# Attention 3: VectorE adds exponentials of two heads, TensorE sums three blocks of denominators per quad in place of six

## The reference

```python
h = jnp.concatenate([x, latents], axis=1)                 # 1601 + 512 = 2113 keys
q = (latents @ q_w + q_b).reshape(b, k_len, NH, DH)       # 512 queries, 16 heads of 32
kv = (h @ kv_w + kv_b).reshape(b, p + k_len, NH, DH, 2)
attn = jnp.einsum('bkhd,bnhd->bhkn', q, kmat) / DH
attn = jnp.where(full_mask[:, None, None, :], attn, -jnp.inf)
attn = jax.nn.softmax(attn.astype(jnp.float32), axis=-1)
attn_out = jnp.einsum('bkhn,bnhd->bkhd', attn, v)
```

## Time and profile before

| | us |
|---|---|
| median of 3 runs | 5292.15 (5284.46 to 5299.27) |
| profiled execution | 5292.46 |
| its span, first to last instruction | 5290.7 |
| PE busy in the span | 4730.2 (89%) |
| DVE busy | 3685.4 (70%) |
| ACT busy | 2956.0 (56%) |
| POOL busy | 2035.2 (38%) |

### The profile page before, as it was taken

The page is one execution under the profiler, slowest core; times in us unless marked ns, Lnnn a source line. Parts: engine busy times, 40 slices in busy tenths (PEclk is TensorE's granted clock), DMA queues, the critical chain, the costliest instruction groups (busy, mean ns, idle before and its releaser), DMA issues. The chain is left out here.

```text
span 5290.7 us, 75559 instructions
## 1 busy us (share of the span) xinstructions
PE 4730.2 (89%) x28874; PEld 1700.7 (32%) x28874; DVE 3685.4 (70%) x4647; ACT 2956.0 (56%) x5454; POOL 2035.2 (38%) x916
## 2 busy tenths in 40 slices
PE   7978898997797999997899999997789999996899
PEld 2423444443333233332322222222333333331344
DVE  6749999997453877771599999994567777771421
ACT  5644444443221466664388888886336666664432
POOL 1226667664000477884000000000008888885000
PEclk9989999998898799998999999998889999998999
DMA  3343434334011333313111111112424232312100
GB/s 129 131 164 105 108 105 125 113 93 152 24 64 43 73 75 74 78 47 109 66 31 32 33 33 34 34 30 71 118 80 99 59 82 58 69 40 77 64 25 16
DMA packets 474866, 391.91 MB, mean 74 GB/s; under 512 B 175151, under 2 KB 372628, under 8 KB 474472
## 3 DMA queue, kind: packets, MB, share of 16 engines
q1 hardware_dynamic: 474496, 387.00, 27.2%
HBM read 246.50 MB, written 139.34 MB: 73 GB/s over the span
## 5 line engine op out<-in xcount | busy, mean ns | idle before, releaser
L2871 DVE TENSOR_REDUCE att_part<-att_scores 128x2 f32<-128x802 f32 x1024 | 953.7, 987 | 110.0 <-PE att_scores L2710 98.1
L2844 ACT ACTIVATE att_prob<-att_lower 128x512 f32<-128x512 f32 (+1 forms) x1664 | 883.2, 596 | 129.6 <-PE att_lower L2724 108.6
L3678 DVE TENSOR_REDUCE att_part<-att_scores 128x1 f32<-128x423 f32 x1280 | 675.8, 590 | 219.5 <-PE att_scores L3381 219.5
L3622 ACT ACTIVATE att_prob<-att_lower 128x512 f32<-128x512 f32 (+1 forms) x1088 | 563.3, 602 | 243.5 <-PE att_lower L3393 241.6
L3662 POOL TENSOR_TENSOR att_acc<-att_acc,att_prob 128x1024 f32<-128x1024 f32 (+2 forms) x240 | 671.4, 2798 | 51.5 <-ACT att_prob L3622 22.4
L2447 DVE TENSOR_REDUCE att_part<-att_scores 128x1 f32<-128x401 f32 x1024 | 515.5, 567 | 162.0 <-PE att_scores L2261 161.9
L1441 POOL TENSOR_TENSOR scan_z<-scan_r,scan_states 128x512 f32<-128x512 f32 x256 | 469.0, 1836 | 337.2 <-DVE scan_states L1518 324.1
L2739 PE MATMUL att_lower<-att_prob,att_v 128*32 128x256 f32 (+1 forms) x6144 | 523.5, 413 | 19.7 <-issue 19.7
L2386 ACT ACTIVATE att_prob<-att_scores 128x512 f32<-128x512 f32 (+1 forms) x832 | 430.9, 601 | 195.6 <-PE att_scores L2273 195.6
L2858 POOL TENSOR_TENSOR att_out<-att_sums_sb,att_spread 128x512 f32<-128x512 f32 x32 | 40.7, 1273 | 1167.4 <-DMA att_spread<-recips 1167.4
L2427 POOL TENSOR_TENSOR att_acc<-att_acc,att_prob 128x1024 f32<-128x1024 f32 (+2 forms) x176 | 450.3, 2559 | 68.6 <-ACT att_prob L2386 56.2
(11 more groups left out here) (435 smaller groups left out, 7912.3 us busy)
## 6 DMA issues: line engine op xcount, KB each, us to landing
v<-scan_val SPq DMA_DIRECT2D x96, 256.0 KB, 2.3
att_v<-v SPq DMA_DIRECT2D x32, 768.0 KB
att_spread<-recips SPq DMA_DIRECT2D x64, 256.0 KB
mix_plane<-in_mask SPq DMA_DIRECT2D x16, 800.5 KB, 8.2
att_k<-k1hi SPq DMA_DIRECT2D x32, 400.2 KB
att_k<-k3hi SPq DMA_DIRECT2D x32, 400.2 KB
scan_x<-in_ctx_t SPq DMA_DIRECT2D x12, 1024.0 KB, 5.9
o<-att_out SPq DMA_DIRECT2D x32, 256.0 KB
```

The lines of the kernel that those rows point to most:

```text
L2844: nc.scalar.activation(prob[g % NP][0:kw(kt), h, :], scores2[0:kw(kt), n % RING2, :], ACT.Exp).then_inc(exped, 1)
L2871: nc.vector.reduce_max(part[q % 2][:, :, ec, piece], scores1[:, bank["unit", p], :, 0:PIECE], AX.X).then_inc(reduced, 1)
L3622: nc.scalar.activation(prob[g % NP][0:kw(kt), h, :], scores2[0:kw(kt), n % RING2, :], ACT.Exp).then_inc(exped, 1)
L3678: nc.vector.reduce_max(part[q % 2][:, hc, piece:piece + 1], scores1[:, bank["piece", p], 0:PIECE], AX.X).then_inc(reduced, 1)
```

## The change

Six key tiles of head 0 (5, 6, 7, 11, 13, 14) and six of head 3 (4, 5, 7, 11, 12, 13) are no longer summed by TensorE. VectorE adds them up in a new tile `acc2`, one 128x512 add for each tile but the first: five per head and quad. The adds of tile t stand in VectorE's program after the reductions of step t+1. After the reductions of step 2 of the next quad one further add, `join`, puts `acc2` onto heads 0 and 3 of `acc`. TensorE's `total` now waits for the join, ScalarE's exponential for the adds that read the tile which it overwrites. TensorE's counts fall from six to three; they stand in steps 5 and 12 and in step 1 of the next quad. GpSimd's adds stay as they are.

```diff
@@ -3085,8 +3085,12 @@
     LEAD, TURN, LAG = 5, 6, 2
     AHEAD = UNITS + LEAD * UNITS // NT
     PADDS = NT - 1
-    FIRST_TOO, LAST_TOO = {13: ((5,), (8,)), 17: ((4, 8, 12), (6, 10, 14))}[NT]
-    counted = {h: [kt for kt in range(2, NT) if kt not in taken] for h, taken in ((0, FIRST_TOO), (QUAD - 1, LAST_TOO))}
+    FIRST_TOO, LAST_TOO = (4, 8, 12), (6, 10, 14)
+    PAIRED = {0: (5, 6, 7, 11, 13, 14), QUAD - 1: (4, 5, 7, 11, 12, 13)}
+    counted = {h: [kt for kt in range(2, NT) if kt not in taken and kt not in PAIRED[h]]
+               for h, taken in ((0, FIRST_TOO), (QUAD - 1, LAST_TOO))}
+    pair_sums = [(h, n, kt) for kt in range(NT) for h in PAIRED for n, t in enumerate(PAIRED[h]) if t == kt and n]
+    SUMS = len(pair_sums)
     COUNTS = len(counted[0]) // 2
     counts = [[(h, kt) for h in counted for kt in counted[h][2 * j:2 * j + 2]] for j in range(COUNTS)]
     counts_at = {max(kt for _, kt in units): j for j, units in enumerate(counts)}
@@ -3094,6 +3098,10 @@
     def counts_to_free(kt):
 
         return max([j + 1 for j, units in enumerate(counts) if min(t for _, t in units) <= kt], default=0)
+
+    def sums_to_free(kt):
+
+        return max([j + 1 for j, (h, n, t) in enumerate(pair_sums) if t <= kt or n == 1 and PAIRED[h][0] <= kt], default=0)
 
     def summed_heads(kt):
 
@@ -3164,6 +3172,7 @@
         V = [ph.sb(f"v{i}", [P, NT, P]) for i in range(2)]
         prob = [ph.sb(f"prob{i}", [P, QUAD, T]) for i in range(NP)]
         acc = [ph.sb(f"acc{i}", [P, QUAD, T]) for i in range(2)]
+        acc2 = ph.sb("acc2", [P, 2, T])
         sums_sb = [ph.sb(f"sums_sb{i}", [P, T]) for i in range(2)]
         den_sb = [ph.sb(f"den_sb{i}", [P, T]) for i in range(2)]
         total_sb = [ph.sb(f"total_sb{i}", [P, T]) for i in range(2)]
@@ -3195,6 +3204,7 @@
         gathered, summed, inverted, parked, broadcast, weighed, normed = (
             ph.sem(n) for n in ("gathered", "summed", "inverted", "parked", "broadcast", "weighed", "normed"))
         biased = ph.sem("biased")
+        pairadded, joined = ph.sem("pairadded"), ph.sem("joined")
         stored = [ph.sem(f"stored{i}") for i in range(2)]
         recips = w["recips"]
         bank = {}
@@ -3417,7 +3427,7 @@
 
                 def total(s):
                     b = take(("total", s), totalout, s + 1)
-                    pe.wait_ge(padded, (s + 1) * PADDS)
+                    pe.wait_ge(joined, s + 1)
                     for h in range(QUAD):
                         ins = nc.tensor.matmul(scores1[32 * h:32 * h + 32, b, :], k["ones"][:, 0:32], acc[s % 2][:, h, :],
                                                start=True, stop=True, tile_position=(0, 32 * h))
@@ -3612,6 +3622,8 @@
                         if os * COUNTS + counts_to_free(ok):
                             act.wait_ge(dendone, os * COUNTS + counts_to_free(ok))
                         act.wait_ge(padded, os * PADDS + max(1, ok))
+                        if os * SUMS + sums_to_free(ok):
+                            act.wait_ge(pairadded, os * SUMS + sums_to_free(ok))
                     if kt == 5 and s:
                         drain_total(s - 1)
                     if kt == 15 and s:
@@ -3688,6 +3700,23 @@
                     if s >= 2:
                         dve.wait_ge(parked, 16 * (s - 1))
                     nc.vector.reciprocal(recip[i][:], folded[i][:, 0, :]).then_inc(inverted, 1)
+
+                def add_pairs(s, kt):
+                    for j, (h, n, t) in enumerate(pair_sums):
+                        if t == kt:
+                            dve.wait_ge(exped, (s * NT + kt) * QUAD + h + 1)
+                            if s and n == 1:
+                                dve.wait_ge(joined, s)
+                            if n > 1:
+                                dve.wait_ge(pairadded, s * SUMS + j)
+                            so_far = prob[(s * NT + PAIRED[h][0]) % NP][:, h, :] if n == 1 else acc2[:, h // 3, :]
+                            nc.vector.tensor_tensor(acc2[:, h // 3, :], so_far, prob[(s * NT + kt) % NP][:, h, :],
+                                                    ALU.add).then_inc(pairadded, 1)
+
+                def join(s):
+                    dve.wait_ge(padded, (s + 1) * PADDS)
+                    dve.wait_ge(pairadded, (s + 1) * SUMS)
+                    nc.vector.tensor_tensor(acc[s % 2][:, 0:QUAD:3, :], acc[s % 2][:, 0:QUAD:3, :], acc2[:], ALU.add).then_inc(joined, 1)
 
                 link = Chain(dve, step)
 
@@ -3775,8 +3804,13 @@
                     while p < pieces_by(g):
                         reduce(p)
                         p += 1
+                    if kt:
+                        add_pairs(s, kt - 1)
+                    if s and kt == 2:
+                        join(s - 1)
                     if g >= NT and kt == 9:
                         invert(s - 1)
+                join(N - 1)
                 invert(N - 1)
         ph.renew()
```

## The result

| | before | changed |
|---|---|---|
| median, us | 5288.56 (4 runs, 5284.46 to 5299.27) | 5714.79 (4 runs, 5701.5 to 5718.39) |
| ratio, 95% interval | 1 | 1.0796 (1.078 to 1.0812) |
| span of the profiled execution, us | 5290.7 | 5713.1 |
| first shift to first matmul of the MLP, us | 915.6 | 1338.6 |
| mean of quads 1 to 13, us | 55.0 | 84.1 |

The change costs 426 us; 344 were forecast. The loop alone grows by 423.0, which is the whole difference of the spans (422.4). So nothing outside attention 3 has to be looked at.

A forecast was written before the change was run, and what follows sets the result against it. The prediction took TensorE, busy for all 55 us of a quad, to bound the kernel. Stalls 318 - 37 counts + 56 clock + 7 end = 344 us more, 5635 us; 8 in 10 for 5450 to 5720.

The forecast's parts named there:

- Counts: Three of six TensorE counts per quad removed, 0.85 us each, over 14.7 quads: 37 us saved.
- the recurrence: Step-by-step timing of attention 3: a score block waits until VectorE's reductions free one of three banks.
- Banks: Adds delaying reductions through three banks, without blocking at SBUF: losses of 1.85, 3.2 and 1.15 us per quad.
- Way to SBUF, steps 6 to 8: VectorE's adds there wait for GpSimd's to end: step 10 begins at 19.61 us instead of 11.36, loss 8.25 per quad.
- Steps 12 to 15: VectorE's adds there wait for GpSimd's: step 17 begins at 26.77 us instead of 15.1, loss 11.67 per quad.
- Join: After step 2's reductions, a 0.1 us race with GpSimd: loss 3.3 us if GpSimd is first, else 1.15; 2.2 taken.
- Clock, 56 us: TensorE at half speed after three pauses per quad, 1.3 us lost each over 14.3 quads; bounds 0 and 100 us.
- End, 7 us: Last quad, paced by GpSimd: ten adds delay it 0.45 us each, a join about 1, then the last join.
- ScalarE's new wait: ScalarE's exponentials waiting for VectorE's adds: costs nothing, since the adds are needed only four steps later.
- Random phases: Rival: adds block, but each group's first add meets GpSimd at a random point: 5530, with clock loss 5585; chance 0.15.
- The second rival: VectorE's adds are not blocked by GpSimd and only the three banks cost time: 5345 us; chance 0.07.
- The third: Rival: VectorE takes the adds in its idle time and TensorE keeps its pace without the counts: 5255; chance 0.04.

The follow-up runs named there:

- x5: Changed kernel without VectorE's adds and join, three counts per quad left, so denominators incomplete: 5256.28 us, 0.9932 of the kernel before.
- x6: Changed kernel with all six counts left in beside the adds and joins, so twelve tiles of two heads count twice: 5713.19 us, ratio 1.0791.
- x1: Changed kernel with VectorE's adds and join replaced by equally long maxima reading one SBUF input: 5352.56 us, 1.0112 of the kernel before.
- x2: Changed kernel with GpSimd's adds of attention 3 cut to 16 of 512 columns, VectorE's adds untouched: 5347.19 us, 1.0099 of the kernel before.
- x4: Changed kernel with matmuls of zeros keeping TensorE busy before the waiting score blocks of steps 7, 9, 13 and 15: 5639.7 us, ratio 1.0659.
- x3: Control: kernel before with GpSimd's adds of attention 3 cut to 16 of 512 columns: 5292.15 us, 0.9995 of the kernel before.
- x7: Changed kernel with the join after the reductions of step 0 in place of step 2: 5635.66 us, 1.0648 of the kernel before.

## Why the prediction was right, and 80 us short

The forecast was +344 in a range from +158 to +428, slower with 0.94; the mechanism, the places and the sign held, and the time lies at the upper edge of the range, 5 us inside it. The steps one by one, against x5's step lengths as the undisturbed ones:

**Counts, -37 us.** Right as a price (x5: -38), and right as a term as long as the losses are counted from steps without these counts, as the recurrence did. It does not say what the counts are worth beside the adds: x6 has them all and takes the same time, 1.0 us more per quad in place of 2.55. That is gain against loss, since the counts also move the meetings, and no rule that a count is free where TensorE waits: steps 13 to 16 lose 2.5 us by them.

**Banks.** Steps 6 to 9 take 13.2 us in x1 and x2 and 11.3 in x5; 1.9 lost, 1.85 forecast. Steps 12 to 16 lose 3.3 in the median (3.2 forecast), steps 3 and 4 1.1 (1.15). The recurrence over three banks was right to 0.1 us in the eight quads of x1 that take about 58.7 us. Its other five take 1.6 us more, and each of them has one stretch of 3.4 us at the low clock.

**Way to SBUF, steps 6 to 8.** With TensorE kept warm (x4) the steps 6 to 9 take 19.59 us; forecast were 19.61. In the changed kernel the first add lasts 3.88 us (3.84 forecast), the lone one of step 7 0.68. The second adds of a pair take 2.64, not 2.8: the hand-over to GpSimd's next add and back costs 0.28 us instead of 0.45. That the sum fits to 0.02 us is luck in part: in x4 the first add of that pair took 2.00 us, not 1.81. The lock itself is shown from both sides, by x1 and x2.

**Steps 12 to 15.** Forecast loss 11.7, in x4 13.2. The forecast let GpSimd begin step 12's add 3.16 us into the step. It left out the multiplication that normalises the quad before (`att_out`), which stands ahead of that add and is in the trace of before too. GpSimd and VectorE in x4, where step 12 begins at 4408.01 us:

```profile
4410.93 1.27 POOL L3662 TENSOR_TENSOR att_out<-att_sums_sb,att_spread 128x512 f32<-128x512 f32 x1
4412.16 6.19 POOL L3679 TENSOR_TENSOR att_acc<-att_acc,att_prob 128x1536 f32<-128x1536 f32 x2
...
4412.47 6.43 DVE L3718 TENSOR_TENSOR att_acc<-att_acc,att_prob 128x512 f32<-128x512 f32 x2
```

GpSimd begins at 4.15, just before VectorE, so the first add takes 3.68 us for 2.63 and the pair ends 0.9 us later than forecast. The rest is argued: step 13 holds the transpose of the maxima, which takes one of the three banks (TensorE's line 3367 in the kernel before), and the recurrence had three there. In x4 the third block of step 13 waits, 0.5 us ahead of the fourth; no run took the transpose or the multiplication out.

**Join.** The race was there: 3.40 us in ten of fourteen joins, 1.22 in four, and 85.3 us per quad with the one, 81.9 with the other. The cheap one costs 1.1 in steps 3 and 4 as forecast, the dear one 4.9 instead of 3.3; I had taken the middle. The 1.6 between is about what 3.4 us at half clock lose (1.7); the clock term had left out the join's pause.

**Clock, 56 us.** This is the term that was most undersized. It took 3.4 us of half clock behind each of three pauses, from the one pause in the earlier trace rows. In the changed kernel it is 27 us of each quad. These are the stretches at the low level in one quad, behind the pauses at the join and in steps 7, 9, 13 and 15, which are 3.1, 2.9, 4.7, 6.1 and 5.2 us long:

```profile
4398.80:4402.20 3.40, 3.40 (x12) 1.12 (x15) 2.08 (x5) 2.35 (x4) 0.94 (x2) 0.50 0.02 5
4415.90:4419.30 3.40, 3.40 (x14) 0.76 (x7) 2.27 (x5) 0.73 (x2) 1.72 (x1) 0.50 0.00 0
4426.10:4432.90 6.80, 5.23 (x17) 1.49 (x18) 4.98 (x9) 1.53 (x3) 0.46 (x1) 0.50 0.02 5
4446.60:4453.40 6.80, 5.08 (x17) 1.18 (x18) 4.75 (x8) 1.74 (x3) 0.61 (x1) 0.50 0.00 0
4460.20:4467.00 6.80, 4.94 (x16) 1.46 (x17) 5.35 (x9) 1.24 (x3) 0.74 (x1) 0.50 0.00 0
```

At each long pause of this quad the clock is low for 6.8 us, twice what the term took; the last 1.6 to 1.9 us of the pause are in it. The two short pauses, for which the term had nothing, are followed by 3.4 us. x4 gives back 75 us and does not get all. Per quad: 84.1 measured, 78.5 forecast (55.0 - 2.55 + 8.25 + 11.67 + 2.2 + 3.9); 2.1 at the least of these 5.6 are the clock (84.1 - 78.05 = 6.0 in place of 1.3 x 3 = 3.9), which leaves 3.5 for the stalls of steps 3, 4 and 12 to 16, with x4's remaining low clock in them.

**End, 7 us.** Size and reason hold for the total. From its first shift to its drained total the last quad takes 64.2 us for 58.0. GpSimd's last add ends 60.2 us after that shift for 55.2, and the join follows it; x3 shows that the total does hang on GpSimd's adds (5.2 us). But GpSimd does not pace the whole quad, as I had it: without its adds the shifts come no faster. I read the pace from the busiest engine, 50.7 of 55 us, and that was no proof.

**GpSimd** gains 25 us in all (769.5 for 744.1 in its four shapes of adds), 1.6 per quad; 5 were forecast. Outside the last quad the time need not show it: in the kernel before a quad takes 55.0 us with GpSimd's long adds and without them (x3). ScalarE's new wait cost nothing, as it was put: no instruction of ScalarE waits for the adds in the changed trace.

**Rivals.** Random phases (5530 to 5585) fell: in the changed kernel, quads with the same kind of join repeat nearly all their meetings to 0.1 us. The second rival is what x1 and x2 are, so the port makes the difference. The third, 5255, is what x5 is: the time the change would have if the adds were free.

## What to carry to other kernels

An engine's idle time in the sum says little about whether work fits: ask what stands behind the new instruction in that engine's queue, who waits for it, and how far the buffers let the waiter run ahead. Where VectorE and GpSimd both add two tiles that lie in SBUF, price the new operation by the rest of the other one's instruction, and look for a form or a place that doesn't meet it (x1 for a form, though its maxima are no sums; x7 for a place). When the stall falls on TensorE, add the slow stretch behind every pause, the short ones too. Look also for the small instructions that shift a meeting, such as the 1.27 us ahead of GpSimd's add of step 12.

## What the runs showed of the hardware

- A VectorE add of two SBUF tiles waits inside the instruction for GpSimd's to end and is counted as busy: 2.1 to 3.9 us for 0.68. A reduction of one SBUF tile at the same places does not: 680 ns in the mean of 160 (x1).
- Two GpSimd adds queued back to back let one VectorE add in between them, so a pair of VectorE adds pays for two GpSimd adds: in 37 of the 39 pairs of quads 1 to 13 the second add took 2.6 to 2.7 us.
- TensorE's granted clock fell to 0.50 for 6.8 us at pauses of 4.7 to 6.1 us, and for 3.4 us behind pauses of 2.9 and 3.1 us. Matmuls of zeros in the pauses kept most of it up (0.96 for 0.84): 6 us per quad won by 74 matmuls more.
